# Loading, transposing and splitting later weights inside the second expert stage

## The reference

```
x = x + 0.5 * moe(layernorm(x))        # 64 experts, top 8, at most 128 rows each, hidden 128
x = x + attention(layernorm(x))        # 16 heads, cumulative-softmax attention
x = x + 0.5 * moe(layernorm(x))        # the same experts again: "second expert stage"
x = x + 0.5 * ffn(layernorm(x))        # weights lut[idx], 688 x 256, 688 x 256, 256 x 688
x = x + hgrn(layernorm(x))             # Wi, Wf, Wg, Wo of 256 x 256
x = x + 0.5 * ffn(layernorm(x))        # the same weights as above
```

## Time and profile before

| | |
|---|---|
| median of 3 runs | 3072.37 us (3071.24 to 3081.69) |
| the profiled execution's own time | 3074.16 us |
| its span in the trace | 3072.5 us |
| PE busy | 2628.7 us (86%) |
| POOL busy | 1405.4 us (46%) |
| DVE busy | 1642.5 us (53%) |
| ACT busy | 909.8 us (30%) |
| mean granted TensorE clock | 0.927 |

### The profile page before, as it was taken

One profiled execution on the slowest core, in us unless ns is written; L12 is line 12 of the kernel. 1 busy time (PEld: TensorE's weight loads), 2 busy tenths in 40 slices (PEclk: granted clock), 3 DMA queues, 4 the chain that ended last, 5 costly groups with the idle time before them and its releaser, 6 DMA issues. The chain is left out here.

```text
span 3072.5 us, 46228 instructions
## 1 busy us (share of the span) xinstructions
PE 2628.7 (86%) x17372; PEld 2264.2 (74%) x17372; DVE 1642.5 (53%) x3218; ACT 909.8 (30%) x1950; POOL 1405.4 (46%) x1386
## 2 busy tenths in 40 slices
PE   5465499999999999999999999965555699796998
PEld 5354388888888888888888888854444577675787
DVE  5332256666666666666666666645221354364543
ACT  5222133333333333333333333334221232121322
POOL 2277545555555555555555555531676111142000
PEclk8688799999999999999999999965898799998999
DMA  6598500000000000000000000026896211111101
GB/s 228 158 246 223 120 8 15 8 8 15 15 8 8 15 15 8 10 13 15 8 11 12 15 8 11 4 84 189 214 219 144 82 62 48 31 59 48 35 28 35
DMA packets 211393, 190.57 MB, mean 62 GB/s; under 512 B 29200, under 2 KB 202224, under 8 KB 210672
## 3 DMA queue, kind: packets, MB, share of 16 engines
q1 hardware_dynamic: 182592, 140.29, 15.2%
q0 software_dynamic: 24576, 37.77, 6.7%
q10 hardware_dynamic: 4016, 9.70, 0.9%
HBM read 121.81 MB, written 65.88 MB: 61 GB/s over the span
## 5 line engine op out<-in xcount | busy, mean ns | idle before, releaser
L1006 DVE TENSOR_TENSOR a_at<-a_psB,causal 128x384 f32<-128x384 f32 x512 | 261.7, 553 | 235.4 <-PE a_psB L1144 226.6
L854 POOL TENSOR_SCALAR a_pick<-a_index,lut_row 128x258 f32<-128x258 int32 x240 | 279.7, 1165 | 24.4
L877 POOL TENSOR_TENSOR a_orstd<-a_ms,minus_half 128x8 f32<-128x8 f32 x64 | 106.8, 1669 | 284.5 <-DVE a_ms L1065 284.5
L601 PE MATMUL e_psX<-ident,e_xg 128*128 128x128 f32 x256 | 62.9, 333 | 182.7 <-DMA e_xg<-rows,slot_tok 182.3
L1032 DVE RECIPROCAL a_rz<-a_psC 128x512 f32<-128x512 f32 x64 | 214.2, 3348 | 0.0
L867 POOL TENSOR_TENSOR a_okn<-a_okn,a_mxs 128x512 f32<-128x512 f32 x64 | 67.0, 1047 | 318.0 <-DVE a_mxs L1039 318.0
L601 PEld LDWEIGHTS e_psX<-ident,e_xg 128*128 128x128 f32 x256 | 32.6, 161 | 230.2 <-DMA e_xg<-rows,slot_tok 225.1
L857 POOL TENSOR_TENSOR a_found<-a_found,a_pick 128x258 f32<-128x258 f32 x240 | 177.4, 739 | 20.0
L956 ACT ACTIVATE a_at<-a_psD 128x512 f32<-128x512 f32 x128 | 76.8, 600 | 369.1 <-PE a_psD L1179 361.0
L694 DVE TENSOR_TENSOR e_hT<-e_psH,e_sil 128x128 f32<-128x128 f32 x128 | 37.3, 291 | 273.4 <-ACT e_sil L662 273.4
L1513 DVE TENSOR_TENSOR f_hs<-f_psU,f_sil 128x512 f32<-128x512 f32 x96 | 66.2, 689 | 218.9 <-PE f_psU L1338 218.9
(11 more groups left out here) (267 smaller groups left out, 8662.5 us busy)
## 6 DMA issues: line engine op xcount, KB each, us to landing
e_wg<-in_L_ffn_w_gate SPq DMA_DIRECT2D x128, 128.0 KB, 3.5
e_wu<-in_L_ffn_w_up SPq DMA_DIRECT2D x128, 128.0 KB, 3.9
e_wd<-in_L_ffn_w_down SPq DMA_DIRECT2D x128, 128.0 KB, 4.4
rows<-r_row SPq DMA_DIRECT2D x32, 320.0 KB, 3.1
stream_b<-r_zeros SPq DMA_DIRECT2D x22, 384.0 KB, 4.7
stream_a<-r_xt SPq DMA_DIRECT2D x32, 256.0 KB, 4.3
r_xt<-in_L_attn_hidden_states SPq DMA_DIRECT2D x16, 256.0 KB, 4.1
a_xab<-stream_a SPq DMA_DIRECT2D x16, 256.0 KB, 2.8
```

Of the source, the lines that this page charges most:

```text
L601: nc.tensor.transpose(psX[u][:, c, :], xg[:, e % U, c * P:(c + 1) * P], cst["ident"][:, :]).then_inc(turned[u], 1)
L854: nc.gpsimd.tensor_scalar(pick[:, :, :], index[:, :, :], float(c), w["lut"][:, c:c + 1], ALU.is_equal, ALU.mult).then_inc(picked, 1)
L877: nc.gpsimd.tensor_tensor(out=flat(orstd[:, :, :]), in0=ms[:, :], in1=cst["minus_half"][:, 0:TT * HQ], op=ALU.pow).then_inc(orstd_ok, 1)
L1006: nc.vector.tensor_tensor(out=at[:, h, :], in0=psB[h % 2][:, 0:3 * P], in1=cst["causal"][:, :, :].rearrange("p a i -> p (a i)"), op=ALU.mu ...
```

## The change

The block of loads and `turn_matrices` are gone. `moe_experts` gets a parameter `turns` with the same 22 groups and the same nine loads, and does both in its second call. SP issues one load behind the weights of each of the experts 2 to 10, now the feed-forward matrices first. PE makes one group behind each second expert from 12 to 54. ACT makes the high part one expert later and DVE the low part (or the copy) two experts later. The groups go through two PSUM tiles of their own. `group_of` gives the same operands as before.

```diff
+        groups, loads = turns if turns else ([], [])
+        if groups:
+            psW = [mem.ps(f"psW{u}", [P, 4 * P]) for u in range(2)]
+            raw_here, raw_turned, high_ok, left_ps = mem.sem("raw_here"), mem.sem("raw_turned"), mem.sem("high_ok"), mem.sem("left_ps")
+        def group_at(e):
+            k, r = divmod(e - 12, 2)
+            return k if e >= 12 and r == 0 and k < len(groups) else None
...
                     sp.dma_start(wd[:, k, :], w_down[e]).then_inc(w_here[k], 16)
+                    if 2 <= e < 2 + len(loads):
+                        sp.dma_start(*loads[e - 2]).then_inc(raw_here, 16)
...
+                def turn_group(k):
+                    high, low, srcs, ps = group_of(k)
+                    pe.wait_ge(raw_here, 16 * len(loads))
+                    if k >= 2:
+                        pe.wait_ge(left_ps, k - 1)
+                    at = 0
+                    for src in srcs:
+                        rows, cols = src.shape
+                        mm = nc.tensor.transpose(ps[:, at:at + rows], src, cst["ident"][0:rows, 0:rows])
+                        at += rows
+                    mm.then_inc(raw_turned, 1)
...
                     if e > 0:
                         result(e - 1)
+                    if group_at(e) is not None:
+                        turn_group(group_at(e))
...
+                    if e > 0 and group_at(e - 1) is not None:
+                        group_high(group_at(e - 1))      # ACT: behind silu and the piece of e
...
+                    if e > 1 and group_at(e - 2) is not None:
+                        group_low(group_at(e - 2))       # DVE: behind weighted(e - 1)
...
-        with nc.Block() as block:
-            @block.sync
-            def _(sp):
-                for k, src in enumerate((Wi1, Wf1, Wg1, Wo1)):
-                    sp.dma_start(h_raw[:, k, :, :], ...).then_inc(h_here, 16)
...
-                sp.wait_ge(h_here, 16 * 9)
-        turn_matrices(nc, "t_", cst, ffn_groups(w_gu, w_dn, wgT, wuT, wdT) + hgrn_groups(h_raw, h_T))
+        loads = []
+        for k in range(2):
+            loads.append((w_gu[k][:, 0:FT - 1, :], looked_up[k][0:(FT - 1) * P, :]...))
+            loads.append((w_gu[k][0:FLAST, FT - 1, :], looked_up[k][(FT - 1) * P:INTER, :]))
+        loads.append((w_dn[:, :, :], looked_up[2]...))
+        for k, src in enumerate((Wi1, Wf1, Wg1, Wo1)):
+            loads.append((h_raw[:, k, :, :], ...))
+        groups = ffn_groups(w_gu, w_dn, wgT, wuT, wdT) + hgrn_groups(h_raw, h_T)
+        moe_experts(nc, cst, "e2_", ..., pool_dma, 1, turns=(groups, loads))
```

More of the change, by code:

```diff
@@ L503, in moe_router, with moe_experts @@
         clear_semaphores(nc, mem)
-def moe_experts(nc, cst, tag, rows, w_gate, w_up, w_down, slot_tok, stream_a, stream_b, pool_dma, run, wide=None, scales_here=None):
+def moe_experts(nc, cst, tag, rows, w_gate, w_up, w_down, slot_tok, stream_a, stream_b, pool_dma, run, wide=None, scales_here=None, turns=None):
     U = 8
@@ L541, in moe_experts, with group_of @@
             pieces = []
+        groups, loads = turns if turns else ([], [])
[5 more added lines that the diff above has]
+            return k if e >= 12 and r == 0 and k < len(groups) else None
+        def group_of(k):
+            high, low, srcs = groups[k]
+            return high, low, srcs, psW[k % 2][0:high.shape[0], 0:high.shape[1]]
         def half_at(e):
@@ L652, in rows_out, with group_high @@
                     nc.scalar.activation(xgT[:, u, :, :], psX[u][:, :, :], ACT.Copy).then_inc(xgT_ok[u], 1)
+                def group_high(k):
+                    high, low, srcs, ps = group_of(k)
+                    if low is not None:
+                        act.wait_ge(raw_turned, k + 1)
+                        nc.scalar.activation(high, ps, ACT.Copy).then_inc(high_ok, 1)
                 rows_out(0)
@@ L687, in weighted, with group_low @@
                     nc.vector.tensor_scalar(y[:, e % W, :], psY[u][:, :], xg[:, k, D + e:D + e + 1], 0.5, ALU.mult, ALU.mult).then_inc(y_ok[u], 1)
+                def group_low(k):
+                    high, low, srcs, ps = group_of(k)
+                    if low is None:
+                        dve.wait_ge(raw_turned, k + 1)
+                        nc.vector.tensor_copy(high, ps).then_inc(left_ps, 1)
+                    else:
+                        dve.wait_ge(high_ok, 1 + sum(groups[i][1] is not None for i in range(k)))
+                        nc.vector.tensor_tensor(out=low, in0=ps, in1=high, op=ALU.subtract).then_inc(left_ps, 1)
                 for e in range(E):
@@ L1847, in macaron @@
         moe_router(nc, cst, "r2_", x_att, gate_w, rows, stream_a, stream_b, slot_tok, counts)
-        moe_experts(nc, cst, "e2_", rows, w_gate, w_up, w_down, slot_tok, stream_a, stream_b, pool_dma, 1)
         w_gu = [mem.sb(f"w_gu{k}", [P, FT, D]) for k in range(2)]
@@ L1855, in macaron @@
         h_T = mem.sb("h_T", [P, 4, DC, D])
-        h_here = mem.sem("h_here")
-        with nc.Block() as block:
-            @block.sync
-            def _(sp):
-                for k, src in enumerate((Wi1, Wf1, Wg1, Wo1)):
[L1861 to L1865, removed]
-                sp.wait_ge(h_here, 16 * 9)
-        turn_matrices(nc, "t_", cst, ffn_groups(w_gu, w_dn, wgT, wuT, wdT) + hgrn_groups(h_raw, h_T))
+        loads = []
+        for k in range(2):
+            loads.append((w_gu[k][:, 0:FT - 1, :], looked_up[k][0:(FT - 1) * P, :].rearrange("(f p) d -> p f d", p=P)))
+            loads.append((w_gu[k][0:FLAST, FT - 1, :], looked_up[k][(FT - 1) * P:INTER, :]))
+        loads.append((w_dn[:, :, :], looked_up[2].rearrange("(c p) o -> p c o", p=P)))
+        for k, src in enumerate((Wi1, Wf1, Wg1, Wo1)):
+            loads.append((h_raw[:, k, :, :], src.rearrange("(r p) n -> p r n", p=P)))
+        groups = ffn_groups(w_gu, w_dn, wgT, wuT, wdT) + hgrn_groups(h_raw, h_T)
+        moe_experts(nc, cst, "e2_", rows, w_gate, w_up, w_down, slot_tok, stream_a, stream_b, pool_dma, 1, turns=(groups, loads))
         lut_ffn(nc, cst, "f1_", [stream_a, stream_b], x_ffn, wgT, wuT, wdT)
```

## The result

The changed kernel took 3059.95 us (median of 7 runs, 3051.26 to 3060.98). The kernel before, run beside it, had a median of 3078.67 us over 7 runs; one of these took 5155.27 us and is left out of the ratio (without it the median is 3076.61 us). The ratio, which compares means, is 0.9941, 95% interval 0.9925 to 0.9957: 18 us (13 to 23) faster. The forecast was -22.0 us and 3050.4 us, with a range up to 3059. So the forecast direction and size lie within the measured interval, but the time itself lies 0.95 us above the top of the range. The profiled execution took 3054.14 us, its span is 3052.4 us: 20.0 us less than the profiled execution before.

The account below looks back on a forecast made before the run. POOL's queue of fetches and scatters, 3.18 us per expert, was taken as the second expert stage's bound. 3074.16 - 26.1 + 0.1 + 4 = 3052.2, less 1.8 to the median: 3050.4 us (-22.0), range 3044 to 3059.

Parts of the forecast that it names:

- Removed work: Behind the second expert stage: without load block and `turn_matrices`, the feed-forward's first load moves from 2405.80 to 2379.68, -26.1 us.
- rival 5: Behind the second expert stage: no gain, as something else holds the feed-forward's start; chance 0.04 together with Rival 4.
- Groups on PE, ACT and DVE: In the second expert stage: transposes and splits fit in idle time and the 7.1 us lead over POOL; cost 0.
- The loads: In the second expert stage: 3.16 MB delay scatter landings, some ten POOL steps at 0.4 us each, +4 us.
- the queue: Loads stand in SP's queue of the weights, not a third one beside POOL's; so 4 us taken, not 8.1.
- Rival 1: Second expert stage: loads cost as on the first stage, 2.7 us per MiB, +8.1 us, 3054.4 us; chance 0.22.
- rival 2: Second expert stage: DMA is the true bound, loads all extra, +12.8 us, 3059.1 us; chance 0.12 with anything beyond.
- rival 3: Second expert stage: the loads are free, 3046.3 us; chance 0.12 of the 0.62 for load costs up to 6.5 us.
- Rival 4: Second expert stage: slower if PE's first group waits for loads landing after 2232; chance 0.04 together with rival 5.
- Two signs: Expected in the second stage's profile: SP's last load issued about 2182; PE's idle time on gathered rows about 10 us shorter.
- the level: Whole kernel's starting time: median 3072.37 us, with the profiled execution of 3074.16 us taken as 1.8 us above it.
- the clock behind the stage: At the feed-forward's start: where PE's clock rises may shift by 1 to 2 us; 2 us put in the range.

Follow-up runs that it names:

- the groups alone: Kernel before with the 22 groups moved into the second expert stage, its nine loads in a block ahead of that stage; ratio 0.9967 to the kernel before.
- the five without loads: Five traces, the kernel before among them, with no extra load in the second expert stage; that stage takes 209.5 us in the mean.
- the spread variant: Changed kernel with the nine loads issued later and apart, behind experts 16 to 37, and groups from expert 18 to 60; ratio 0.9936 to the kernel before.

## Why the prediction was right about the change and wrong about the time

**Removed work, -26.1 us.** Right: -25.8 us. The start of the feed-forward hangs on nothing else (rival 5 is out). The passage left is 10.30 and 10.22 us where 10.0 to 10.1 was forecast; the four more semaphores may account for the 0.2 to 0.3 us, which no run tested.

**Groups on PE, ACT and DVE, 0 us.** Right, shown by the groups alone. With them inside, the granted clock was no lower over the stage: 0.93 and 0.92 from 2170 to 2371 in the two traces of the changed kernel, against 0.92 and 0.90 in the two of before. It fell for a while around the first groups, to 0.72 from 2204 to 2214 (before: 1.00), and no scatter was held by that. DVE's splits beside POOL cost nothing either: no scatter of the stage lasted above 1.63 us.

**The loads, +4 us.** Right in size: 4.1 us in the mean of two traces (3.4 and 4.8 us over the five without loads). The mechanism is what was named (a scatter that lands late holds the one two behind it). That the product came out so well is in part luck, since its factors were off: ten steps at 0.4 us each were forecast, and the first trace has its excess in six steps, up to 4.5 us long, 5.5 us above 3.19 in sum, where the two traces of before have 0.8 and 1.7 us there (4.9 us once in the second changed trace, and up to 4.9 us behind a large load further on). Waiting for a better moment inside the stage would not have helped. What sets the price is in the main whether the loads are long or cut small, which the sum did not have; the queue, the reason for taking a low value, is not shown to matter. Rival 1's price (8.1 us) and rival 2's (12.8 us) are excluded for SP's queue, and rival 3's zero as well. Rival 4, PE late for the first group, did not occur: the idle time ahead of L645 is 0.0.

**Two signs were off.** SP's last load went out at 2189.6, not 2182, because the weights of experts 8 to 10 stand ahead of it and wait, and the stage began 3.4 us later; it landed at 2196.8. PE's idle time on gathered rows fell by 4.5 us (84.8 to 80.3), not by 10; the stage itself had got longer.

**The step that failed is the level, not the effect.** "That execution was 1.8 us above the median of 3072.37, so the forecast is 3050.4" took three runs as the kernel's level. The full set of before, to which these three belong, has a median of 3078.67 us (3076.61 without the run of 5155.27), and later sets had 3077.73, 3077.09, 3081.16 and 3077.94 us: 4 to 9 us higher. -22 us from 3076.61 is 3054.6, inside the range. The miss is 9.6 us: 4.2 us are the level, and 5.3 us the difference of medians, 16.7 us where 22.0 was forecast. That second part is not shown to be an error of the sum, as the interval of the gain (13 to 23 us) holds 22, and the traces of stage and passage give 21.9 us in the mean. The range had 2 us for the clock behind the stage, a value that no row was shown for, and nothing for the spread of the program: the 64 undisturbed runs of before lie between 3066.49 and 3090.29 us, and the untouched first expert stage alone varies by 12 us. The three runs shown (3071.24 to 3081.69) had already given a hint, one of them 9 us up.

**What stays open.** The two traces of the changed kernel say -22.6 and -21.3 us, the two timings -18 and -20. The variants' timings lie up to 5 us to either side of their traces, so this is within what one trace can tell, and I can't say whether 2 us of the gain are lost elsewhere. What makes the first expert stage wander was not tried; it has nine loads of 1 MiB beside POOL's scatters, which is the mechanism above at three times the bytes, but that is an argument and no result.

## What to carry to other kernels

Serial load-and-prepare work between stages goes well inside a stage that is paced by another engine's issue rate: engines with idle time took it for nothing. The bytes are the part to be careful with. Where an engine's queue waits for its own earlier DMA to land, a large transfer beside it costs time that never comes back, so put the loads where DMA is idle, or cut them small: here each took away most or all of the 4.1 us. Measure a stage from a mark that the change and chance leave alone; the first scatter was none. And give a forecast of absolute time the spread of the whole program, not that of the passage under study.

## What the runs showed of the hardware

- In the spread variant two of three loads of 640 or 688 KB beside GpSimd's indirect scatters lengthened one step from 3.19 to 4.8 or 4.9 us, the third to 3.63; behind loads of 256 KB the steps were 3.2 to 3.63 us.
- The same 3.02 MiB cost the stage 4.1 us as nine loads of up to 688 KB (two traces), 8.1 us with twice the bytes, and 0.9 us as 24 loads of at most 172 KB (one trace each).
- The price of the same loads was 1.4 us per MiB in SP's queue and 2.0 in ACT's, over 209.5 us without them. That is one trace against two, with other moments of issue. The Trainium skill ("DMA: Bandwidth & Descriptors", section "Issuing engines are not separate DMA queues") says that the issuing engine makes no difference to where a DMA runs; the traces don't speak against that, and a larger delay of the third party with ACT's queue is not shown.
- An unaltered stage with heavy DMA beside indirect scatters took 219.14 to 231.49 us in twelve traces, a width of 12.4 us; the attention stage behind it, from its first load to the router's, 1670.8 to 1676.8 us.
